# Feed-forward of a pre-norm transformer layer: two tiles of three split in rows and turned by a transfer, the products of the others two turns later

## The reference

```
x = x + attention(layernorm(x))
h = layer_norm(layernorm(x)) @ ternary(w1).T + b1      # 128 -> 512
h = gelu(h)
h = layer_norm(h)                                       # over 512
x = x + h @ ternary(w2).T + b2                          # 512 -> 128
```

## Time and profile before

| | |
|---|---|
| median of 3 runs | 995.39 us (995.16 to 996.04) |
| profiled execution | 993.86 us, of it 992.1 span |
| busy in the span | PE 969.8 (98%), DVE 854.8, ACT 732.8, POOL 861.5 |
| granted PE clock | 0.998 |
| first hidden product | 873.96 |
| gelu of tile 12 / of tile 60 | 901.68 / 978.59 |
| last instruction | 992.1 |

### The profile page before, as it was taken

How to read it: one execution, slowest core, us unless ns; L and a number is a source line. 1 busy time by engine, 2 the same in 40 slices (tenths; PEclk the granted TensorE clock), 3 DMA queues, 4 the chain that set the end, 5 groups by cost and what they waited for, 6 DMA issues and landing times.

```text
span 992.1 us, 39212 instructions
## 1 busy us (share of the span) xinstructions
PE 969.8 (98%) x15932; PEld 768.5 (77%) x15932; DVE 854.8 (86%) x1743; ACT 732.8 (74%) x1180; POOL 861.5 (87%) x849
## 2 busy tenths in 40 slices
PE   7899999999999999999999999999999999989998
PEld 6577777787787887887778788777778877767776
DVE  6888988888888898889888898899888988768877
ACT  4687777778777777777777777787777777767775
POOL 5789898989886998999989998999899989888875
PEclk9999999999999999999999999999999999999999
DMA  6212232232322343223334232233333433367985
GB/s 136 44 31 53 47 75 51 62 63 63 79 43 51 63 84 64 63 52 54 85 62 63 63 80 38 62 58 84 63 63 64 63 64 63 69 133 148 180 171 129
DMA packets 242786, 74.08 MB, mean 75 GB/s; under 512 B 218032, under 2 KB 240304, under 8 KB 242608
## 3 DMA queue, kind: packets, MB, share of 16 engines
q1 hardware_dynamic: 240528, 71.05, 36.6%
q10 hardware_dynamic: 2080, 0.52, 0.3%
HBM read 11.41 MB, written 8.39 MB: 20 GB/s over the span
## 4 chain that ended last, share of the span: by engine, by line
PE 90%; DVE 2%; ACT 2%; DMA 2%; issue 2%; SPq 1%; POOL 1%; DVEq 0%; ACTq 0%
PE S L765 11%; PE PV L790 8%; PE M L725 7%; PE PV L792 6%; PE PV L791 6%; PE QK L713 5%; PE QK L712 5%; PE QK L714 5%; PE misc L765 5%; PE S L757 5%; PE M L843 2%; PE M L808 2%; PE M L844 2%; PE M L845 2%; PE misc L757 2%; PE M L810 2%
## 5 line engine op out<-in xcount | busy, mean ns | idle before, releaser
L1325 POOL TENSOR_TENSOR pl<-p 128x1024 f16<-128x1024 f32 x253 | 476.3, 1894 | 33.3 <-ACT p L1102 33.1
L1526 DVE TENSOR_REDUCE negmax<-M 128x4 f32<-128x1024 f32 x252 | 306.8, 1217 | 22.2 <-PE M L725 16.1
L1110 ACT ACTIVATE QKh<-QK 128x512 f16<-128x512 f32 x251 | 149.4, 595 | 142.5 <-PE QK L714 141.7
L1102 ACT ACTIVATE p<-S,s_exp 128x1024 f32<-128x1024 f32 x173 | 192.0, 1110 | 56.9 <-PE S L765 56.4
L790 PEld LDWEIGHTS PV<-V,p 128*128 128x128 bf16 x2048 | 186.6, 98 | 47.1 <-issue 36.3
L790 PE MATMUL PV<-V,p 128*128 128x65 f16 x2048 | 214.9, 193 | 4.5 <-DVE O L1540 3.6
L791 PE MATMUL PV<-V,p 128*128 128x64 f16 x2048 | 213.2, 193 | 0.0
L792 PE MATMUL PV<-V,pl 128*128 128x65 f16 x2048 | 212.5, 194 | 0.0
L1546 DVE TENSOR_TENSOR QKl<-QK,QKh 128x512 f16<-128x512 f32 x251 | 172.4, 687 | 43.1 <-ACT QKh L1110 42.0
L791 PEld LDWEIGHTS PV<-V,p 128*128 128x128 bf16 x2048 | 189.0, 97 | 4.7
L792 PEld LDWEIGHTS PV<-V,pl 128*128 128x128 f16 x2048 | 188.7, 97 | 0.0
(11 more groups left out here) (246 smaller groups left out, 2473.7 us busy)
## 6 DMA issues: line engine op xcount, KB each, us to landing
y_kept<-yTb SPq DMA_DIRECT2D x32, 128.0 KB, 1.7
yT<-y_kept SPq DMA_DIRECT2D x16, 256.0 KB, 3.3
result<-X SPq DMA_DIRECT2D x15, 256.0 KB, 2.9
X<-in_L_attn_query SPq DMA_DIRECT2D x7, 512.0 KB, 4.4
OT<-O SPq DMA_TRANSPOSE x64, 4.0
shift<-negmax SPq DMA_TRANSPOSE x63, 2.3
O<-in_L_attn_Wk ACTq DMA_DIRECT2D x2, 256.0 KB, 4.8
O<-in_L_attn_Wq SPq DMA_DIRECT2D x2, 256.0 KB, 5.5
```

The source lines that it names most:

```text
L1102: e.activation(p32[r][:, :, :, :].rearrange("p i m n -> p (i m n)"), score_bank(p)[:, :], ACT.Exp, scale=s_exp[:, :]).then_inc(s_ex, 1)
L1325: e.tensor_tensor(pl[r][:, :, :, :].rearrange("p i m n -> p (i m n)"), p32[r][:, :, :, :].rearrange("p i m n -> p (i m n)"), p_high(r).rea ...
L1526: e.tensor_reduce(dst[:, :, NB * jj:NB * jj + NB], max_bank(p)[:, :].rearrange("p (i t m) -> p i t m", i=2, t=NB), AX.X, ALU.max, negate=T ...
```

## The change

`in_rows` takes two tiles of three (i mod 3 = 0 or 1, below 60) in place of the even ones: 40 row tiles in place of 30, 24 bank tiles in place of 34. `out_turn` is i + 15 for every tile below 60, so the products of a bank tile come two turns later. The wait of `turn_z` for its slot is written by the list of row tiles; the tile three places before is now 4 or 5 tiles back, where it was always 6.

```diff
 def in_rows(i):
-    return i % 2 == 0 and i < ROWS_END
+    return i % 3 != 2 and i < ROWS_END

 def rows_no(i):
-    return i // 2
+    return sum(in_rows(k) for k in range(i))

 def out_turn(i):
-    return i + (L_OUT_ROWS if in_rows(i) else L_OUT)
+    return i + (L_OUT_ROWS if i < ROWS_END else L_OUT)

+ROWS = [i for i in range(NT) if in_rows(i)]

                 if n >= 3:
-                    e.wait_ge(s_f, OUT_NO[i - 6])
+                    e.wait_ge(s_f, OUT_NO[ROWS[n - 3]])
```

## The result

The changed kernel takes 999.40 us in the median of 7 runs (998.62 to 1001.01), the one before 995.39 beside it (994.16 to 996.73): ratio 1.0043, 95% interval 1.0033 to 1.0053, so +3.3 to +5.3 us. The forecast was 998.8. The profiled execution took 998.62, of it 996.6 span, 4.5 more than before.

A forecast was written before the change was run, and what follows sets the result against it. PE's own work and the yT load chain, two loops of 9.21 and 9.16 us per six turns, were taken as the bound. Stage +1.5, start +1.2 and end +0.7 gave +3.4 on 995.39: 998.8 us, range 993.5 to 1003.

The forecast's parts named there:

- The bound of the kernel before: Feed-forward, tiles 12 to 60: PE's work (9.21 us per six turns) and the yT load loop (9.16) bind; 3.2 lost.
- The root between two low parts, a seven-turn loop of 11.99: POOL, each third group: the root delays tile 4g-6's low part and so tile 4g's load; stage +1.5 us.
- PE's 4.3 us: PE: ten fewer tiles to transpose save 4.3 us, most of it not to be had because of the load loop.
- DVE and ACT at nothing: Ten low parts leave DVE, ACT's copies change source, sums wait for products: cost 0, bounds 0 to +0.5 us.
- SP and DMA at no extra delay: Ten more transposing transfers: DMA asks for 17.8 of 19.0 us per twelve turns, no extra delay; least evidence.
- rival C: DMA engines saturate, landings 0.7 to 1 us later for two of three groups; 1004.8 us, chance 0.18.
- allowance for long issues and landings: Stage: long issues hitting a loop without slack in two of three groups, 1.8 us, and spread of landings, about 0.5.
- ACT's new wait at 0: ACT waits for a zp slot freed by the transfer four turns back; just fits, cost 0, bound +2 us.
- Start +1.2: Feed-forward start: tile 3's low part on POOL delays attention's last O and the load; tile 8 1.2 us later.
- End +0.7: After the last load PE has nine sets of output products left instead of eight: +0.7 us.
- The stalls every twelfth tile: PE's waits for yT grow, concentrated at tiles 16, 28, 40 and 52, 1 to 1.5 us each.
- Rivals A and B: A: PE's saving comes through, 992.9 us, chance 0.18. B: POOL's sum alone bounds, 994.8 us, chance 0.22.

The follow-up runs named there:

- before_load5: The kernel before with the load of yT issued one turn earlier (L_LOAD 5 for 6); 990.91 us, 0.9955 of the kernel before.
- turn_only: The kernel before with only the change's second half: every second tile in rows, all products below tile 60 at turn i + 15; 995.66 us, ratio 1.0001.
- after_load5: The changed kernel with the load of yT issued one turn earlier (L_LOAD 5 for 6); 1.0026 of the kernel before.
- after_end: The changed kernel with the products of bank tiles 56 and 59 back at i + 13; 1.0039 of the kernel before.

## Why the prediction was right, and where its working was not

The forecast was +3.4; measured +4.3 (3.3 to 5.3). That the sum came so near is in part luck: the start was put 0.6 too high, the end 1.4 and the stage 0.3 too low, and an effect that it did not name, the lower clock, stands in the start. By its steps:

- **The bound of the kernel before**: two loops of 9.21 and 9.16 per six turns. Right: before_load5 took the waits away and gave back 4.5 us, 2.35 of them seen in the stage, where 3.2 had been counted.
- **The root between two low parts, a seven-turn loop of 11.99**: right where the chain shows it (12.11 at tile 52), low elsewhere (12.56, 12.81), and back at 11.9 to 12.5 with the bias left out or with four slots. In the case of 12.81 the low part of tile 34 started at 941.80, S+5.47, as worked out; 0.7 came later in the issue of its transfer (1.90 for 1.23), one of the long issues that the forecast had counted apart, and 0.2 in the store, which waited for DVE's sum. In the case of 12.56 the low parts were late by 0.4, behind an instruction that the forecast's sum for POOL leaves out: the low part of `y`, 0.67 us, which POOL still has at 918.25. Stage +1.5 forecast, +1.84 measured. Moving the root shortened the three loops by 0.4 to 0.7, less than the 1.7 it takes, and the kernel not at all.
- **PE's 4.3 us**: in the stage, with eight of the ten tiles, 3.4 were due and PE was busy 2.4 less (72.72 for 75.13), while its waits for `yT` and `zT` rose by 4.3. So the saving was lost to waits, as said.
- **DVE and ACT at nothing**: the moved products alone cost nothing measurable (turn_only 1.0001). But DVE now waits 11.9 us for PE's products ahead of its sums, where before it had no such wait, and 0.2 us of the loop of tile 40 came from there, within the bound of 0.5.
- **SP and DMA at no extra delay**: this step failed. Eight transfers alone cost 1.7 us, and DMA share rose to 0.92. PE also got waits for `zT` that the forecast hadn't named, 2.2 us ahead of the stage, 1.0 in it and 0.6 behind; how much of these is the transfers' and how much that of late low parts is open. It was not as rival C has it: landings were to be 0.7 to 1 us later, and in the stage the medians rose by 0.1. The forecast may have escaped because its allowance for long issues and landings (1.8 + 0.5) stood where this belonged, and because PE's saving covers part of the sum of both additions (3.8 + 1.7 = 5.5 alone, 4.3 in the change); no run shows this.
- **ACT's new wait at 0**: right, 6.3 us off the path.
- **Start +1.2**: the number is near, the path is another. The last `O` moved by 0.90 and the landing of the load by 0.55, as the mechanism asks. But what held tile 8 was PE itself, which had waited 2.17 us for the first turned tile and then ran for 3.4 us at half the clock. Tile 8 moved by 0.98, and 0.4 of it was given back by tile 12.
- **End +0.7**: mis-sized, +2.06. The ninth set of products is there; a second cause, the bank slot of tile 59, was missed (2.26 on ACT; without both the end takes 14.78 for 16.43), and PE waited 0.63 for `zT` after tile 60.
- **The stalls every twelfth tile**: half right. Tiles 28, 40 and 52 have 0.49, 1.17 and 0.93 on the matmul rows, tile 16 none; tile 24, of a group with g mod 3 = 0, has 1.18, the longest. The forecast had set these groups aside as 0.38 over inside the same loop. Here POOL had had hardly a break since 904.2, with a root last, and began the low part of tile 18 3.8 us behind its hidden product in place of 2.62.
- **Rivals A and B**: out. The saving of PE did not come through, and POOL's sum alone (17.8 per twelve turns) was not what bounded them: the twelve turns from tile 16 on were 20.7, 20.7 and 19.1.

Open: how the 4.3 us divide between POOL and the transfers inside the change (the two added alone sum to more), and what the stretch at the lower clock costs in the time, as it stands in some of the profiled executions of the changed kernels and not in others.

## What to carry to other kernels

When an engine is at 98% but the pace of its work is slower than its own instructions, look for a second loop of the same length through other queues, and shorten that one first: here one issue moved by a turn was worth 4.5 us, and ten tiles' transposes taken off the busiest engine, at the price of ten low parts and ten transfers, lost 4.3. Work moved from a full engine to one with 13 us of idle time costs where it stands in front of something, so list what is queued behind it. After each relief ask what is next: here the next bound was 2 us away and had another name.

## What was not expected of the hardware

POOL's idle time was no reserve for the loop: eight instructions of 1.15 us, with nothing depending on them, cost 3.8 us, 0.47 each. Eight transposing transfers of 128x1024 16-bit elements with no reader cost 0.2 us each while the DMA engines were at 0.86; in after_load5 the engines showed 1.01 over 76.5 us, with single microseconds above 2, and the median landing of `zT` grew from 3.4 to 3.8. A wait of 2.17 us on PE was followed, 1.2 us after its end, by 3.4 us at a granted clock of 0.5; waits of 2.24 in after_load5 and 2.31 in after_end were not.
